# Layer 3's experts on sorted tiles of token-expert pairs, in a four-layer attention and expert kernel

## The reference, cut to what matters

```python
gates = jax.nn.softmax(xf @ _wn(gate_v, gate_g).T + gate_b, axis=-1)
_, top_idx = jax.lax.top_k(gates, 2)
out = jnp.zeros_like(xf)
for i in range(E):                       # E = 8
    mask = jnp.any(top_idx == i, axis=1).astype(xf.dtype)[:, None]
    W1 = _wn(w1_v[i], w1_g[i])           # row / norm * gain
    h = (xf * mask) @ W1.T + b1[i]
    h = h * jax.nn.sigmoid(h)
    W2 = _wn(w2_v[i], w2_g[i])
    out = out + mask * (h @ W2.T + b2[i])
```

## Time and profile before

| | us |
|---|---|
| median of 3 runs (1088.66 to 1089.29) | 1088.7 |
| the profiled execution | 1088.03 |
| its span, first to last instruction | 1086.0 |
| PE busy in the span | 876.1 (81%) |
| DVE busy | 587.1 (54%) |
| ACT busy | 410.0 (38%) |
| POOL busy | 252.9 (23%) |
| mean granted TensorE clock | 0.882 of full speed |

### The profile page before, as it was taken

The page is one execution under the profiler, slowest core; times in us unless marked ns, Lnnn a source line. Parts: engine busy times, 40 slices in busy tenths (PEclk is TensorE's granted clock), DMA queues, the critical chain, the costliest instruction groups (busy, mean ns, idle before and its releaser), DMA issues. The chain is left out here.

```text
span 1086.0 us, 15074 instructions
## 1 busy us (share of the span) xinstructions
PE 876.1 (81%) x5302; PEld 604.8 (56%) x5302; DVE 587.1 (54%) x1280; ACT 410.0 (38%) x763; POOL 252.9 (23%) x288
## 2 busy tenths in 40 slices
PE   6895889839984744787789689996999888689998
PEld 4673445429972524775478323232566677557776
DVE  5784535446546575447668577761544548522111
ACT  3340535533341300353434146764322334243443
POOL 0543300100043203544735331010000114310110
PEclk9996879978986965798889869998899989978999
DMA  7005231053514000110000504100010100001100
GB/s 326 2 14 133 65 99 25 2 230 87 157 55 166 2 0 20 39 55 1 1 1 2 136 11 140 37 2 0 15 44 29 54 1 1 1 1 39 39 29 31
DMA packets 33247, 56.82 MB, mean 52 GB/s; under 512 B 3696, under 2 KB 25392, under 8 KB 32784
## 3 DMA queue, kind: packets, MB, share of 16 engines
q1 hardware_dynamic: 31712, 52.98, 15.7%
q0 software_dynamic: 1472, 3.02, 1.0%
HBM read 46.41 MB, written 10.35 MB: 52 GB/s over the span
## 5 line engine op out<-in xcount | busy, mean ns | idle before, releaser
L1593 DVE TENSOR_REDUCE arena<-psum 128x2 f32<-128x1024 f32 (+3 forms) x128 | 127.1, 1021 | 76.5 <-PE psum L2297 47.7
L1103 ACT ACTIVATE arena<-psum 128x512 f32<-128x512 f32 (+3 forms) x256 | 115.8, 515 | 82.5 <-PE psum L2310 45.7
L2585 PE MATMUL psum<-xT_all,wexp 128*128 128x512 f32 x272 | 125.3, 605 | 0.9 <-ACT arena L1204 0.6
L778 POOL TENSOR_TENSOR rstd<-var,held 128x8 f32<-128x8 f32 (+3 forms) x22 | 46.1, 2104 | 256.9 <-DVE var L1348 234.6
L2294 PE MATMUL psum<-arena 72*128 72x512 bf16 (+3 forms) x256 | 82.0, 392 | 25.4 <-DMA arena<-parts_q 12.5
L2222 PE MATMUL psum<-values_out_all,arena 128*128 128x128 f32 x560 | 76.8, 285 | 26.7 <-ACT arena L1067 26.0
L853 POOL TENSOR_TENSOR arena<-arena,small 128x616 f32<-128x616 f32 x56 | 68.0, 1217 | 126.8 <-DVE small L1525 126.5
L1964 DVE SCALAR_TENSOR_TENSOR x_res<-psum,arena,x_res 128x128 f32<-128x128 f32 x136 | 38.3, 344 | 101.8 <-PE psum L2600 101.7
L2222 PEld LDWEIGHTS psum<-values_out_all,arena 128*128 128x128 f32 x560 | 67.6, 193 | 36.3 <-ACT arena L1067 35.0
L2307 PE MATMUL psum<-arena 75*128 75x512 bf16 (+3 forms) x256 | 75.7, 361 | 7.5 <-DMA arena<-arena 6.0
L1054 ACT ACTIVATE arena<-arena 128x616 f32<-128x616 f32 x56 | 40.2, 717 | 108.2 <-DVE arena L1521 108.2
(11 more groups left out here) (335 smaller groups left out, 1602.3 us busy)
## 6 DMA issues: line engine op xcount, KB each, us to landing
wexp<-experts SPq DMA_DIRECT2D x16, 514.0 KB, 3.6
arena<-experts SPq DMA_DIRECT2D x16, 514.0 KB, 4.0
parts_k<-wexp SPq DMA_DIRECT2D x12, 384.0 KB, 2.9
arena<-parts_k SPq DMA_DIRECT2D x48, 96.0 KB
arena<-parts_q SPq DMA_DIRECT2D x48, 96.0 KB
arena<-rows SPq DMA_DIRECT2D x8, 512.0 KB, 7.9
wexp<-experts SPq DMA_DIRECT2D x9, 384.0 KB, 3.0
held<-packed SPq DMA_DIRECT2D x1, 2375.0 KB, 16.0
```

Source lines behind the costliest of these rows:

```text
L778: pool.tensor_tensor(dst, src, half[0:src.shape[0], 0:n], ALU.pow).then_inc(done, 1)
L1103: act.activation(p_self[:, n % 2, kt % 2, j, lo:S], bank(t_bank("keys", c, k), lo, S), ACT.Exp, scale=DS ** -0.5).then_inc(ut_ok, 1)
L1593: dve.tensor_reduce(top[:, x % 2, qt, j:j + 2], src, AX_X, ALU.max, negate=True).then_inc(us_ok, 1)
L2585: mm(bank(c, 0, BANK), wexp[:, side, c * P:(c + 1) * P], xT_all[:, b * S:(b + 1) * S], start=True, stop=True).then_inc(h_ps, 1)
```

## The change

Layer 3's experts take layer 1's way, with two pairs to a token: 2048 pairs in 2048/128 + 7 = 23 tiles. `queues1`, `places1`, `places_in_tiles` and `experts1` become `sorted_experts(l)` and `places(l)` for both layers; the dense loop, `experts3` on POOL, and the loads of layer 3's experts in pairs go. The normalised tokens are written to DRAM twice (once for each choice), and 23 tiles are fetched, computed and scattered. All eight experts' weights are loaded into `arena` once layer 3's attention no longer needs the place; each expert's slab is 1160 wide and holds the inverse norms beside the weights: ACT takes the first layer's as a scale with its bias, DVE multiplies the answer by the second's row instead of copying it. The norms are combined (POOL) and the diagonal blocks written (DVE) during layer 3's attention. Running sums over tiles are by doubling (three additions for layer 1, four for layer 3). The output leaves in two DMAs.

```diff
+TOPK = {1: 1, 3: 2}
+TILES = {l: TOPK[l] * B * S // P + 8 - 1 for l in TOPK}
+STRIDE = {1: 1028, 3: 1160}
...
-            sp.dma_start(tokens_in[B * S:ROWS_OUT, :], zeros).then_inc(cleared, 16)
+            for l in SORTED:
+                sp.dma_start(tokens_in[l][TOPK[l] * B * S:ROWS_OF[l], :], zeros[0:TILES[l] * P, :]).then_inc(cleared, 16)
...
+            def sorted_experts(l):
+
+                sp.wait_ge(x_xTp, B * (l + 1))
                 for e in range(8):
-                    sp.dma_start(R["w"][:, e * 1028:(e + 1) * 1028], experts[1][e]).then_inc(w0_in[e % 4], 16)
...
+                    first = e * STRIDE[l]
+                    sp.dma_start(R[l]["w"][:, first:first + 1028], experts[l][e]).then_inc(w0_in[e % 4], 16)
+                src = r_res if l == 1 else xn_moe
+                sp.wait_ge(m_xn, B * (l + 1))
+                for k in range(TOPK[l]):
+                    sp.dma_start(tokens_in[l][k * B * S:(k + 1) * B * S, :].rearrange("(t p) d -> p t d", p=P),
+                                 src[:, 0:NT * P].rearrange("p (t d) -> p t d", d=P)).then_inc(sent, 16)
                 for side in range(4):
-                    sp.wait_ge(d_back[side], BACK0 + 16 * len(range(side, TILES1, 4)))
+                    sp.wait_ge(d_back[side], BACK0 + 16 * side_total(l, side))
...
+                    for k in range(TOPK[l]):
+                        first = k * B * S + b * S
+                        sp.dma_start(R[l]["back"][:, first:first + S].rearrange("p (t d) -> p t d", d=P),
+                                     sorted_out[l][first:first + S, :].rearrange("(t p) d -> p t d", p=P))\
+                          .then_inc(d_stored[b * TOPK[l] + k], 16)
...
-            block_done(sp, 8)
-            sp.dma_start(out.rearrange("(t p) d -> p t d", p=P),
-                         x_res[:, :].rearrange("p (t d) -> p t d", d=P)).then_inc(stored, 16)
-            sp.wait_ge(stored, 16)
...
+            for b in range(B):
+                sp.wait_ge(f_done, 2 + b)
+                sp.dma_start(out[b * S:(b + 1) * S, :].rearrange("(t p) d -> p t d", p=P),
+                             x_res[:, b * S:(b + 1) * S].rearrange("p (t d) -> p t d", d=P)).then_inc(stored, 16)
...
+                if l == 3:
+                    row_norms3()
                 pool.memset(E4[l][:, :, HALF:CHUNKED], 0.0).then_inc(pads_ok, 1)
...
-                for j in range(TILES1):
+                for j in range(n):
                     deliver(j)
-                    if j + 8 < TILES1:
+                    if j + 8 < n:
                         fetch(j + 8)
...
             def row_norms3():
 
+                held_in(pool, 4)
                 pool.wait_ge(n_inv, 3)
-                pool.tensor_tensor(s1_all, s1_all, w("m3_g1"), ALU.mult)
+                pool.wait_ge(x_xTp, 4 * B)
...
+                        kw = dict(bias=r["w"][:, bass.ds(at + (1024 + c), 1)])
+                        if l == 3:
+                            kw["scale"] = r["w"][:, bass.ds(at + (1028 + c), 1)]
...
+                    if l == 3 and n in (4, 6):
+                        norm_rows3(n // 2 - 2)
...
+            def cleared_ahead():
+
+                for name in ("m12", "pre", "mk"):
+                    last = dve.memset(M[name][:, 0:64], 0.0)
+                step.then(last)
...
+                cur = M["m12"]
+                ahead = [1, 2, 4, 8][0:3 if n == 8 else 4]
+                for i, d in enumerate(ahead):
+                    dst = M["pre"] if i % 2 else M["mk"]
+                    last = dve.tensor_tensor(dst[:, 64:64 + N], cur[:, 64:64 + N], cur[:, 64 - 8 * d:64 + N - 8 * d], ALU.add)
...
-                step.then(dve.memset(pre[:, 0, :], 0.0))
-                for t in range(1, NT):
-                    step.then(dve.tensor_tensor(pre[:, t, :], pre[:, t - 1, :], m[:, t - 1, :], ALU.add))
...
+                    if l == 3:
+                        ins = dve.tensor_tensor(dst, src, r["w"][:, bass.ds(first_of[j] + 1032, P)], ALU.mult)
...
+                    for k in range(TOPK[l]):
+                        side = b * TOPK[l] + k
...
+                        ins = dve.tensor_tensor(a, a, r["back"][:, k * B * S + b * S:k * B * S + (b + 1) * S], ALU.add)
```

More of the change, by code:

```diff
@@ L76, in constants @@
         "before": np.triu(np.ones((P, P), f)),
+        "after": np.triu(np.ones((P, P), f)) - 1,
         "firstness": np.broadcast_to(16.0 - np.arange(16, dtype=f), (P, 16)),
@@ L296, in program @@
         Z = take(dict(lane=1024, which=2 * 24 * 8, off=24, row=24, at=16, first=16))
-        R = take(dict(past_M=12032, xin=8 * P, xe=2 * P, h=2 * 512, y=4 * P, gap=608, w=8 * 1028))
-        back1 = M["s"][:, 0:NT * P]
+        Z = take(dict(lane=1024, which=2 * 24 * 8, off=24, row=24, at=16, first=16, past=192, sq=192))
+        R = {1: take(dict(past_Z=4096, back=NT * P, past_M=6912, xin=8 * P, xe=2 * P, h=2 * 512, y=4 * P, gap=608, w=8 * STRIDE[1])),
+             3: take(dict(past_Z=1872, xe=2 * P, h=2 * 512, y=4 * P, xin=8 * P, back=2 * NT * P, diag=8 * P, gap=6640,
+                          w=8 * STRIDE[3]))}
+        assert all(sum(v.shape[-1] for v in r.values()) == ARENA for r in R.values())
         lane_of = Z["lane"].bitcast(BF16).rearrange("p (n c) -> p n c", c=P)
@@ new lines, in _ @@
+            sorted_experts(1)
+            n = MOE[2]["E"] + 1
+            sp.wait_ge(ye_ps, 2 + KB[2])
+            selfattn(1)
+            with sp.Fori(0, (n - 2) // 2) as i:
+                for side in range(2):
+                    sp.wait_ge(ye_ps, i * 4 + (2 + KB[2] + 2 * side + 2))
+                    load(2, i * 2 + (side + 2), side)
+            sp.wait_ge(ye_ps, 2 + KB[2] + 2 * (n - 2))
+            load(2, n - 1, 0)
+            sorted_experts(3)
+            for b in range(B):
+                sp.wait_ge(f_done, 2 + b)
+                sp.dma_start(out[b * S:(b + 1) * S, :].rearrange("(t p) d -> p t d", p=P),
+                             x_res[:, b * S:(b + 1) * S].rearrange("p (t d) -> p t d", d=P)).then_inc(stored, 16)
@@ L765, in _ @@
+            sp.wait_ge(stored, 32)
         @block.gpsimd
@@ L1861, in places1 @@
+                step.then(dve.tensor_scalar(row, blocks_, float(P), -float(P), ALU.mult, ALU.add))
                 step.then(dve.tensor_tensor(row, row, lanes, ALU.add))
                 dve.tensor_tensor(row_i[:, 0:24], row, off, ALU.add).then_inc(slots_ok, 1)
-                step.then(dve.tensor_tensor(e8(M["mk"][:, 128:192]), e8(w("r_within")), each, ALU.mult))
-                step.then(dve.tensor_reduce(ended, e8(M["mk"][:, 128:192]), AX_X, ALU.add))
-                past = M["h"][:, 2048:2240].rearrange("p (j e) -> p j e", e=8)
+                step.then(dve.tensor_tensor(blocks(sq[2]), blocks(w("r_within")), each, ALU.mult))
@@ L1866, in places1 @@
+                step.then(dve.tensor_reduce(ended, blocks(sq[2]), AX_X, ALU.add))
+                past = Z["past"].rearrange("p (j e) -> p j e", e=8)
                 step.then(dve.tensor_tensor(past, ended.unsqueeze(1).broadcast_to([P, 24, 8]),
@@ L1891, in experts1 @@
+                    ins.then_inc(d_y, 1)
+                places(l)
+                dve.wait_ge(tiles_ok, turn_of(l) + 1)
+                weights_in(dve, l)
+                if l == 3:
+                    dve.wait_ge(n_s2, 2)
                 features(0)
                 features(1)
-                for j in range(TILES1):
-                    if j + 2 < TILES1:
+                for j in range(n):
+                    if j + 2 < n:
                         features(j + 2)
```

351 lines of the change are left out of this document (178 added, 173 removed).

## The result

The changed kernel's median is 1047.9 us (four runs, 1044.33 to 1049.39) against 1088.7 for the kernel before, a ratio of 0.962 (95% interval 0.9594 to 0.9646). The forecast was 1045.9, with a range of 1042.0 to 1051.8. The profiled execution took 1044.33 us, its span 1042.5; the sum had given 1045.2 and 1043.2.

A forecast was written before the change was run, and what follows sets the result against it. TensorE bound the dense experts; POOL's issues were to pace the new loop. First fetch 972.06, first delivery 983.15, last 1030.9, end 1042.9, elsewhere +0.3: span 1043.2, profiled 1045.2, median 1045.9 us, range 1042 to 1051.8.

The forecast's parts named there:

- diagonal blocks in the attention: DVE's eight blocks moved into layer 3's attention: between 0 and 1.6 us, taken as 0.8.
- sums over partitions: Layer 3's planning on PE: 1.8 us from layer 1's 1.63, bounds 1.63 and 3.3.
- 15 pairs: Layer 3's loop, POOL alternating delivery and fetch: 2.583 us a pair, 38.74 in all.
- TensorE's 1.89 us a tile: Layer 3's tiles: TensorE's need for 17 matmuls at full clock, read from layer 1's 54 matmuls in 6.00 us.
- The first rival: TensorE sets the loop's pace: 41.6 us in place of 47.7, whole time 1039.8 us; chance 0.05.
- expected sign of a POOL-paced loop: In layer 3's loop TensorE idles some 0.7 us a tile, waiting for fetched rows or free answer places.
- Serialised DMAs: In the loop each indirect DMA issue waits for the previous landing: 5.5 us a pair, whole time 1100 us; chance 0.03.
- The clock at half throughout: TensorE at half clock in the loop: 75 us in place of 47.7, whole time 1073 us; chance 0.05.
- Copies that hold descriptors: DVE's weight copies delay POOL's DMA issues: 2.95 to 2.98 us a pair, whole time 1051.6 us; chance 0.05.
- the tail: Behind the last delivery: 2.38 us to the loads, 2.96 to DVE's addition, 3.0 for four additions, 3.6 for output.
- From the profiled execution to the median: Last step of the whole-time sum: 0.67 us added to the profiled 1045.2, giving 1045.9.
- The second rival: TensorE's clock stays at half in the loop: 3.4 us a tile, whole time 1073 us; chance 0.05.

The follow-up runs named there:

- second trace: Trace of the changed kernel executed once more with no edit; six executions had a median of 1045.6 us.
- same kernel again: The changed kernel executed once more with no edit; median 1045.6 us (1039.47 to 1048.37).
- the same half and no late fetches: Changed kernel without layer 3's fetches of tiles 8 to 22 and without half its tiles' matmuls; first to last delivery 37.9 us against 48.0.
- the run with the most added matmuls: Changed kernel plus unread matmuls in layer 3's planning, six behind the turned gates, two behind the biases; first fetch to last delivery 58.6 us.

## Why the prediction was right, and where it was not

By its own steps, in us, from the changed kernel's first trace:

| step | forecast | measured |
|---|---|---|
| ahead of layer 3's first score sum | -0.5 | -0.8 |
| diagonal blocks in the attention | +0.8 | +1.77 |
| last attention addition to the bias (12.32 before) | +0.25 | +0.31 |
| two choices and running sums | 4.1 | 4.2 |
| sums over partitions | 1.8 | 1.0 |
| slots | 6.7 | 6.6 |
| row numbers | 2.6 | 2.6 |
| first fetch to first delivery | 11.1 | 10.4 |
| 15 pairs | 38.7 | 39.0 |
| last pair to last delivery | 9.0 | 9.0 |
| loads, additions | 5.3 + 3.0 | 5.2 + 4.0 |
| output | 3.6 | 2.7 |

How near the sum comes is in part luck. The first row is a draw from the scatter ahead of layer 3: in the second trace the score sum starts 2.6 us later than in the kernel before, not 0.8 earlier. Of the other rows five miss by 0.7 to 1.0, three one way and two the other. In the prediction's own arithmetic two slips change nothing: its high ends add up to 1052.7, not 1051.5 (it says that not all come at once), and the 948.64 of its first step stands in none of its rows; it is about the end of POOL's operation ahead of that norm.

**The bound.** POOL's issues set the loop, as forecast; leaving out half of TensorE's work and doubling DVE's copies left it where it was. That layer 1 could be read for layer 3 term by term held because the instructions are the same, and POOL's pace hardly depended on what stood beside it: 38.7 to 39.0 us for the 15 pairs in the changed kernel, with half of TensorE's matmuls, and with twice DVE's copies.

**TensorE's 1.89 us a tile** was the step that failed within it. It was read from the end of layer 1's tiles, where ACT applies a function with a bias alone; the scale that the change adds was given 0.1 us once, in the first tile, while it costs ACT 0.36 in every tile, and 0.16 of that came back as TensorE's pace (2.12 against 1.96); the other 0.07 over 1.89 stayed open. The price of the scale stood in the trace of the kernel before, 779 against 597 ns. The first rival was priced at 41.6 for the loop and is in truth 46.7. The expected sign of a POOL-paced loop, TensorE idle for some 0.7 us a tile, was therefore absent, and the margin of the forecast was 1.3 us, not 6. Both lids being so near, the time hardly shows which one holds: had TensorE set the loop at its real pace, the forecast would have come out as well.

**The diagonal blocks** were bounded by their own 1.6 us and put at 0.8, on the idea that DVE's wait of 1.05 would take some. They cost 1.77, above the upper bound. In either group of four one block lasts about as long as POOL's operation beside it (1307 ns at the most, where the median is 275; the first group is on from 896.76, POOL from 896.92), and with POOL idle the four took 0.87. The Trainium skill, "SBUF — State Buffer", section "Who interferes with whom", states this: a DVE operation in a mode that uses two ports (tensor_scalar is one that can) and a GpSimd operation cannot hold the shared ports at once, and the loser waits for a whole instruction. The rows agree. The prediction cited that rule for POOL's descriptors, where the second copy showed nothing (39.04 against 39.02), and did not use it in the place where it acted.

**The other rivals.** Serialised DMAs: pairs of 2.60, gaps of 0.30 that are not waits. The clock at half throughout: 1.00 from 983 on. Copies that hold descriptors: a second copy a tile added 0.02 us to 39.

**Sums over partitions and the tail** missed by 0.8 to 1.0 each and cancelled. The row behind the sums was read at half clock: in layer 1 of the kernel before TensorE's granted clock is 0.50 from 430 to 434, in layer 3 of the changed kernel 1.00 from 961 to 964, where two matmuls of 128x128 take 0.47 us against 0.67 for two of 128x64 there. In the tail the third and fourth load did land late, by the 0.86 and 0.17 that DVE waits; the last output half left sooner, 2.7 us to the end.

**From the profiled execution to the median** was the largest miss, and no row could have told it: 0.67 us was taken from the kernel before, it was 3.5 here. In the same kernel again the profiled execution took 1048.27 and lay 2.6 above the median of 1045.6. It is a draw from the scatter ahead of layer 3.

## What to carry to other kernels

When a stage is handed from one engine to a loop that several share, write down each engine's time per turn with the operands that the new code has, not those of the place it was read from: a scale added to ACT's operation came back in part as TensorE's pace. Where two lids stand within a few per cent, neither busy shares nor the chain of waits told which one holds; the gaps in POOL's own timeline pointed to it, and taking work from each engine, and from both, showed it. Small work that is moved into a busy stage belongs where its own engine waits; beside a neighbour that shares its ports its price is not bounded by its own busy time (1.77 us for 1.6).

## What the runs showed of the hardware

With half of its matmuls left out, TensorE did not keep its clock in the tiles. In that run's stretches

```profile
985.00:1005.00 20.00, 13.79 (x85) 10.74 (x86) 10.08 (x29) 14.36 (x39) 15.29 (x16) 0.98 0.18 53
1015.00:1025.00 10.00, 8.39 (x33) 6.81 (x33) 4.20 (x13) 5.76 (x16) 7.60 (x8) 0.50 0.18 55
```

the same work a tile is done at 2.4 GHz at first and at 1.2 GHz later, and the last delivery waits for its answer, so that the seven behind the pairs take 9.9 us against 9.0. The second rival was thus nearer than it looked: with its real 2.1 to 2.2 us a tile TensorE kept 1.00 in the changed kernel, with half of the matmuls at POOL's pace it did not. With the same half and no late fetches, where the tiles come faster, it did (1.00 from 985 to 1010, busy 20.09 of 25 us). And in the run with the most added matmuls it stood at 0.50 from 979 to 985 while TensorE was busy 5.83 of 6 us.
